# A one-core graph kernel whose edge-count stage is regrouped: five items to a PSUM group, twenty to a set

## The chip, the cores and the metric

The kernel runs on one core of one Trainium2 chip. The metric is device time in microseconds (us) of one execution. The engines are TensorE (PE; its weight loads are listed apart as PEld), VectorE (DVE), ScalarE (ACT), GpSimd (POOL) and the DMA queue that SyncE (SP) issues. TensorE's clock has two levels, 2.4 GHz (granted clock 1.0) and 1.2 GHz (0.5).

## What is computed

Four graph layers run over 3125 nodes with 96 features and 100000 edges, sorted by destination. Every layer reads neighbours only through sums over edges, so the kernel first builds the dense matrix of edge counts and then uses it in all layers:

```python
edge_index = jnp.stack([src, dst])
h = jnp.maximum(_layernorm(x, axis=-1), 0.0)
x = x + _L0_gnn_ref(h, qW, kW, vW, src, dst)            # attention over edges
h = jnp.maximum(_layernorm(x, axis=-1), 0.0)
x = x + _L1_gnn_ref(h, p_t, Wv, bv, edge_weight, edge_index)
h = jnp.maximum(_layernorm(x, axis=-1), 0.0)
x = x + _L2_gnn_ref(h, src, dst, W, b)                  # segment_sum(h[src], dst)
h = jnp.maximum(_layernorm(x, axis=-1), 0.0)
x = x + _L3_gnn_ref(h, edge_index, ...)                 # Chebyshev propagation
# inside L1: a softmax of edge_weight over the edges of one target
seg_max = jax.ops.segment_max(edge_weights, tgt, num_segments=n)
e = jnp.exp(edge_weights - seg_max[tgt])
denom = jax.ops.segment_sum(e, tgt, num_segments=n)
gamma = e / denom[tgt]
```

The change touches only the first stage, which builds the counts `CT` and, beside it, the softmax of the edge weights.

## The kernel before

**The count stage.** The edges lie in 782 chunks of 128, the destinations in 784 windows of `W = 4`. Since the edges are sorted, chunks and windows cross in a staircase of `NI = 1565` items, each one chunk against one window. For an item, VectorE makes two one-hot tiles from the edges' keys (`one_hots`, L408): `oneS`, 128 edges by 128 low parts of the source, and `mov`, 128 edges by 25*4 = 100 columns (high part of the source, destination in the window). TensorE multiplies them (L516), which gives the counts of that item. **A group** is 4 items in a row: they accumulate in one PSUM bank, 25 blocks of 16 columns, each item at an offset that comes from a register. A fifth matmul with the identity (L520, 400 columns) adds what `CT` already holds there, and ScalarE copies the bank back into `CT` (L559). The staircase is cut in two halves, `LH = 792` items apart, and groups g and g+1 belong to different halves, so that only g and g+2 touch the same place: the identity matmul of g waits for the copy of g-2 (semaphore `placed`). There are 392 groups.

**Sets and registers.** A set is two groups, 8 items, whose one-hots are made by one pair of VectorE instructions; there are `SETS = 198`, in `DEEP = 3` buffers: the one-hots of set s wait until set s-3 is counted. The window offsets lie in a small table `wI` in SBUF. Before every fourth group TensorE and ScalarE each execute a TENSOR_LOAD (`load_windows`, L455): 16 words on TensorE, 4 on ScalarE. I call the four groups between two loads a quad.

**What feeds the keys.** Items come in blocks of 128 slots (`NJ = 13`). For block j GpSimd gathers the chunks by indirect DMA (L207, L210), VectorE splits the source (`high`, L416 and L419), GpSimd makes the keys (`keys`, seven instructions, L217 to L229), TensorE transposes them (`turn_items`) and ScalarE stores them (`keep_items`, L543). Tables of numbers say after which set each of this happens (`TURN_AT`, `HIGH_AT`). Where an item's chunk lies is found by comparing slot numbers with the chunks' last windows: VectorE's `past` (L302 for block 0, L433 for the other twelve, in sets 0 to 3) and sums on TensorE (`later_sums`, L476, after sets 3, 4 and 5, 28 matmuls each).

**The softmax** runs on VectorE in 12 steps, one after every eighth set (`SOFT_AT`), each a run of several instructions over 128x782 elements (`soft_step`, L355).

**The start.** `CT` (39350 f32 words a partition) must be zero before the first group; GpSimd, VectorE and ScalarE share that (`ZG1` to `ZA`), and TensorE waits for the semaphores `zero_g`, `zero_v` and `zero_a`. A second iota, `iotaS` for blocks 1 to 12, is written by GpSimd at L234.

After the stage all engines meet (`meet`), and projection, attention, propagation and the last layer follow.

Of the kernel before, what the change touches and what calls it, by code (L numbers as in the profile page):

```python
# [15 lines left out]
NP = 3136  # L16
# [4 lines left out]
NC = 782  # L21
# [3 lines left out]
LH = 792  # L25
NW = NP // W
NI = NC + NW - 1
NJ = 13
# [78 lines left out]
TURN_AT = {14 if j == 1 else 16 * (j - 1) + 6: j for j in range(1, NJ)}  # L107
HIGH_AT = {12 if j == 1 else 16 * (j - 1) + 1: j for j in range(1, NJ)}
SOFT_AT = {24 + 8 * k: k for k in range(1, 13)}


PAST_AT = {0: (0, 1), 1: (2, 3), 2: (4, 5), 3: (6,)}
SUM_AT = {3: range(1, 5), 4: range(5, 9), 5: range(9, NJ)}
SLOTS_AT, TABLE_AT = 8, 10
KA = 5


def items_of(g):
# [10 lines left out]
def keys_of(K, j):  # L129
    return K.KLa[:, j, :, :, :] if j < KA else K.KLb[:, j - KA, :, :, :]  # L130


def alloc_build(K, st):
# [4 lines left out]
    K.KLa = sb(st, "KLa", [128, KA, 2, 128, 2], I16)  # L138
# [23 lines left out]
    K.oneS = sb(st, "oneS", [128, DEEP, 8, 128], F16)  # L162
    K.mov = sb(st, "mov", [128, DEEP, 8, 25 * W], F16)
    K.cs = sb(st, "cs", [128, 4], F32)

    with ExitStack() as st2:
        K.iotaS = sb(st2, "iotaS", [128, SLOTS], I16)
        K.past = sb(st2, "past", [128, 7, SLOTS], F16)
    K.KLb = sb(st, "KLb", [128, NJ - KA, 2, 128, 2], I16)
# [1741 lines left out]
```

## Time and profile before

| | |
|---|---|
| median of 3 runs | 1454.96 us (1450.79 to 1456.13) |
| the profiled execution's own time | 1454.33 us |
| its span in the trace | 1452.3 us |
| PE, DVE, ACT, POOL busy over the span | 79%, 69%, 49%, 37% |
| the count stage in it, first matmul on `oneS` to the last copy | 29.1 to 416.9 us |

The time of an execution holds the span and 2.0 us around it. Busy shares are averages over stages with different limits, so the count stage has to be read by itself: in what rhythm its groups follow one another, and what ends each pause.

### The profile page before, as it was taken

The page shows a single profiled execution, that of the slowest core. Times are in us where ns is not written, and L with a number is a line of the kernel's source. Part 1 is how long each engine was busy: PE and PEld are TensorE (multiplying, and loading weights), DVE is VectorE, ACT ScalarE, POOL GpSimd, SP SyncE. Part 2 cuts the span into 40 slices and gives each one's busy share as a digit, 9 for nine tenths or more (in the row PEclk, how much of TensorE's full clock was granted, in tenths as well). Part 3 has the DMA queues.
Part 4 walks back from the last instruction along what each step waited for, and adds up shares of the span by engine and source line. Part 5 has one row for each costly group of instructions (what it writes and reads, how often), then busy time and mean ns, then how long its engine had stood idle before and what let it go on. Part 6 is the DMA issues. An engine that isn't in the chain of part 4 may idle for free.

```text
span 1452.3 us, 24477 instructions
## 1 busy us (share of the span) xinstructions
PE 1142.7 (79%) x8411; PEld 676.2 (47%) x8411; DVE 1008.8 (69%) x1873; ACT 717.7 (49%) x986; POOL 538.7 (37%) x325
## 2 busy tenths in 40 slices
PE   2877876787769947788787877788479699999994
PEld 1555554555535412122222222222368697778783
DVE  7678788766653438989998999887775554432376
ACT  6555554555532149989997989987100000001121
POOL 6521211221000063989997999887000000000000
PEclk9857666776658959999998999999589899999996
DMA  0100000000013311111111121111111100010111
GB/s 4 55 10 5 5 5 5 16 8 1 1 35 84 95 42 30 43 42 45 44 43 39 32 59 47 50 45 38 50 42 50 37 29 8 1 28 8 50 36 34
DMA packets 61187, 47.32 MB, mean 33 GB/s; under 512 B 31216, under 2 KB 59504, under 8 KB 60944
## 3 DMA queue, kind: packets, MB, share of 16 engines
q1 hardware_dynamic: 59440, 44.04, 10.8%
q0 software_dynamic: 1632, 1.72, 0.5%
q8 instruction: 76, 1.25, 0.4%
q14 instruction: 39, 0.32, 0.1%
HBM read 31.94 MB, written 13.79 MB: 31 GB/s over the span
## 4 chain that ended last, share of the span: by engine, by line
PE 52%; DVE 23%; ACT 15%; issue 6%; POOL 2%; another core or an unknown queue 1%; DMA 0%; ACTq 0%; SPq 0%; DVEq 0%
PE PS L1312 16%; DVE Eb L1118 12%; PE PS L516 10%; PE PS L520 8%; ACT Eb L1083 5%; ACT Eb L1085 5%; ACT CT L559 3%; PE PS L1032 3%; PE PS L1668 3%; PE PS L852 2%; PE PS L1021 2%; PE PS L1042 1%; PE PS L836 1%; POOL Eb L959 1%; DVE Eb L1112 1%
## 5 line engine op out<-in xcount | busy, mean ns | idle before, releaser
L959 POOL TENSOR_SCALAR Eb<-Eb 128x1024 f32<-128x1024 f32 (+4 forms) x164 | 405.1, 2484 | 71.6 <-ACT Eb L1087 71.2
L1118 DVE SCALAR_TENSOR_TENSOR Eb<-Eb,PS 128x1024 f32<-128x1024 f32 (+4 forms) x350 | 365.0, 1083 | 51.6 <-ACT Eb L1085 38.9
L516 PE MATMUL PS<-mov,oneS 128*128 128x100 f16 x1565 | 220.1, 257 | 93.2 <-ACT CT L559 70.9
L559 ACT ACTIVATE CT<-PS 128x400 f32 x392 | 197.6, 504 | 185.7 <-PE PS L520 176.4
L1312 PE MATMUL PS<-hs,CT 128*128 128x192 f16 (+3 forms) x2500 | 270.2, 272 | 6.0 <-DVE B L1513 2.7
L1087 ACT ACTIVATE Eb<-PS,small 128x1024 f32<-128x1024 f32 (+5 forms) x257 | 247.2, 995 | 35.2 <-PE PS L1032 22.6
L1312 PEld LDWEIGHTS PS<-hs,CT 128*128 128x128 f16 (+1 forms) x2500 | 233.5, 101 | 39.2 <-DVE B L1513 3.2
L516 PEld LDWEIGHTS PS<-mov,oneS 128*128 128x128 f16 x1565 | 160.4, 115 | 176.5 <-DVE mov L408 109.0
L1032 PE MATMUL PS<-Qb,Kb 96*128 96x512 f16 (+3 forms) x700 | 202.4, 372 | 25.7 <-ACT Eb L1087 9.9
L520 PE MATMUL PS<-CT,identb 128*128 x392 | 182.6, 466 | 0.9 <-ACT CT L559 0.8
L1042 PE MATMUL PS<-Eb,V 128*25 128x512 f32 (+3 forms) x1400 | 174.8, 572 | 2.1 <-DVE Eb L1118 2.0
L1021 PE MATMUL PS<-identb,CT 128*128 128x128 f16 (+1 forms) x625 | 69.9, 228 | 87.5 <-DVE Eb L1118 83.5
L408 DVE TENSOR_TENSOR oneS<-iotaX,KLb 128x1024 f16<-128x1024 int16 x118 | 82.7, 701 | 66.4 <-PE PS L520 65.4
L1032 PEld LDWEIGHTS PS<-Qb,Kb 96*128 96x128 f16 (+1 forms) x700 | 47.6, 100 | 161.7 <-ACT Eb L1087 84.6
L1021 PEld LDWEIGHTS PS<-identb,CT 128*128 128x128 f16 (+1 forms) x625 | 40.7, 101 | 163.3 <-DVE Eb L1118 149.6
L1083 ACT ACTIVATE Eb<-PS,small 128x1024 f32<-128x1024 f32 (+4 forms) x93 | 102.8, 1105 | 25.8 <-PE PS L1032 14.5
L1513 DVE TENSOR_REDUCE SG<-PS 128x96 f32<-128x288 f32 (+3 forms) x75 | 30.1, 420 | 104.7 <-PE PS L1312 104.3
L1085 ACT ACTIVATE Eb<-Eb,small 128x1024 f32<-128x1024 f32 (+4 forms) x93 | 97.6, 1050 | 3.0
L222 POOL TENSOR_SCALAR key<-hi 128x128 f32<-128x128 int32 x13 | 8.2, 627 | 238.0 <-DVE hi L416 237.8
L1406 ACT ACTIVATE hs<-PS 96x96 f32<-96x96 f32 x9 | 2.2, 248 | 179.1 <-PE PS L1333 179.1
L408 DVE TENSOR_TENSOR oneS<-iotaX,KLa 128x1024 f16<-128x1024 int16 x80 | 56.6, 708 | 38.0 <-PE PS L520 28.9
L1112 DVE TENSOR_SCALAR Eb<-Eb 128x1024 f32<-128x1024 f32 (+4 forms) x93 | 66.2, 712 | 20.3 <-ACT Eb L1087 11.1
(270 smaller groups left out, 1096.1 us busy)
## 6 DMA issues: line engine op xcount, KB each, us to landing
Kb<-kd SPq DMA_DIRECT2D x168, 96.0 KB
qd<-QH SPq DMA_DIRECT2D x24, 96.0 KB, 2.0
kd<-QH SPq DMA_DIRECT2D x24, 96.0 KB, 2.2
XG<-x_d SPq DMA_DIRECT2D x12, 192.0 KB, 2.4
x_d<-XG SPq DMA_DIRECT2D x12, 192.0 KB, 1.9
hs<-t_d SPq DMA_DIRECT2D x12, 192.0 KB, 2.5
Qb<-qd SPq DMA_DIRECT2D x4, 384.0 KB, 3.7
CT<-x_d SPq DMA_DIRECT2D x1, 1200.0 KB, 7.8
```

The lines of the kernel that those rows point to most:

```text
L516: t.matmul(to, K.oneS[:, s % DEEP, 4 * r + k, :], K.mov[:, s % DEEP, 4 * r + k, :].rearrange("p (a w) -> p a w", a=25), start=(k == 0), st ...
L520: t.matmul(ps, K.identb[:, :], K.CT[:, :, bass.ds(vals[0], 4 * W)], start=False, stop=True, skip_group_check=True).then_inc(S("counted"), 1)
L559: a.activation(K.CT[:, :, bass.ds(vals[0], 4 * W)], K.bank(g % 4)[:, 0:25 * 4 * W].rearrange("p (a c) -> p a c", a=25), ACT.Copy).then_inc ...
L959: g.tensor_scalar(e, e, ELO, None, ALU.max).then_inc(S("floored"), 1)
L1021: m = p.transpose(K.cntv[it % 2][0:r, 128 * i:128 * i + w], K.CT[0:w, B0[b] + i, 128 * t:128 * t + r], K.identb[0:w, 0:w])
L1032: m = p.matmul(bank(h)[0:r, 0:wb], K.Kb[:, it % NK, h, 0:r], K.Qb[:, b % 2, h, 0:wb], start=True, stop=True)
L1042: m = p.matmul(bank(4)[32 * h:32 * h + 25, 0:wb], K.V[0:r, t, h, :], K.Eb[0:r, (2 * it + h // 2) % NE_, h % 2, 0:wb], start=(t == 0), stop ...
L1083: a.activation(e, ps, ACT.Relu, bias=K.ten[0:r, 0:1], scale=K.unsc[0:r, :]).then_inc(S("score_read"), 1)
L1085: a.activation(e, e, ACT.Exp, bias=K.ten[0:r, 1:2]).then_inc(S("exp_a"), 1)
L1087: a.activation(e, ps, ACT.Exp, scale=K.unsc[0:r, :]).then_inc(S("score_read"), 1)
L1118: v.scalar_tensor_tensor(out=e, in0=e, scalar=EHI, in1=cn, op0=ALU.min, op1=ALU.mult).then_inc(S("weighed"), 1)
L1312: m = p.matmul(bank(t % FIRST)[0:r, 0:w], K.CT[:, a, 128 * t:128 * t + r], hs[:, a, :, :].rearrange("p k d -> p (k d)"), start=(a == 0), s ...
```

## The change

A group is five items now and a set four groups, twenty items (`GI = 5`, `SET = 20`). The identity matmul has 500 columns, the copy 128x500, the one-hot instructions 128x2560 and 128x2000. There are 313 groups in 80 sets, with two buffers in place of three. A register load belongs to one set: 20 words for four groups of five. A block is 120 slots, and there are 14; the keys lie in a ring of 4 blocks. The wait for `placed` of g-4 is gone (that of g-2 stands). The softmax is dealt out in 27 single pieces by a table of gaps. The comparisons are made in three parts (block 0, blocks 1 to 7, blocks 8 to 13), the second of them before the count loop; the large iota stands before the first gather, where a zeroing of 2000 words stood, and the zeroing shares are new. The halves are `LH = 795` apart.

```diff
-LH = 792
+LH = 795
-NJ = 13
+NJ = 14
-SETS = 198
-SLOTS = NJ * 128
-PRESENT = [g for g in range(2 * SETS) if 4 * (g // 2) + LH * (g % 2) < NI]
-DEEP = 3
-SOFT_AT = {24 + 8 * k: k for k in range(1, 13)}
+GI = 5
+SETS = 80
+SET = 4 * GI
+BLOCK = 6 * SET
+SLOTS = NJ * BLOCK
+PRESENT = [g for g in range(4 * SETS) if GI * (g // 2) < (LH, NI - LH)[g % 2]]
+DEEP = 2
+RING = 4
+HIGH_AT = {3 if j == 1 else 6 * (j - 1) + 1: j for j in range(1, NJ)}
+TURN_AT = {4 if j == 1 else 6 * (j - 1) + 3: j for j in range(1, NJ)}
+PARTS = ((0, 1), (1, 8), (8, NJ))
+PAST_AT = {0: (0, 1, 2, 3), 1: (4, 5, 6)}
+SUM_AT, SLOTS_AT, TABLE_AT = 2, 5, 7
+SOFT_GAPS = (1, 1, 1, 3, 3, 1, 1, 1, 3, 3, 1, 3, 1, 3, 3, 1, 1, 1, 3, 3, 1, 1, 1, 1, 3, 3, 1)
+SOFT_AT = {16 + sum(SOFT_GAPS[:k]): k for k in range(len(SOFT_GAPS))}
...
-ZG1, ZG2, ZG3 = 2000, 5500, 12500
-ZV = ZG3 + 6500
-ZA = ZV + 15000
+ZG1, ZG2 = 3500, 10500
+ZV = ZG2 + 4500
+ZA = ZV + 18500
...
-    g.memset(K.CTf[:, 0:ZG1], 0.0).then_inc(S("zero_g"), 1)
+    g.iota(K.iotaS[:, BLOCK:SLOTS], [[GI, 12 * (NJ - 1)], [LH, 2], [1, GI]], base=GI * 12, channel_multiplier=0,
+           allow_small_or_imprecise_dtypes=True).then_inc(S("iota"), 1)
...
     gather(0)
-    g.memset(K.CTf[:, ZG1:ZG2], 0.0).then_inc(S("zero_g"), 1)
-    g.iota(K.iotaS[:, 128:SLOTS], [[4, SLOTS // 8 - 16], [LH, 2], [1, 4]], base=4 * 16, channel_multiplier=0,
-           allow_small_or_imprecise_dtypes=True).then_inc(S("iota"), 1)
+    g.memset(K.CTf[:, 0:ZG1], 0.0).then_inc(S("zero_g"), 1)
     keys(0)
-    g.memset(K.CTf[:, ZG2:ZG3], 0.0).then_inc(S("zero_g"), 1)
     g.wait_ge(S("slot_w"), 2)
     gather(1)
+    g.memset(K.CTf[:, ZG1:ZG2], 0.0).then_inc(S("zero_g"), 1)
...
+    soft = softmax_pieces(v, K)
     for s in range(SETS):
-        j, o = s // 16, 8 * (s % 16)
+        j, o = s // 6, SET * (s % 6)
         v.wait_ge(S("items"), j + 1)
         if s >= DEEP:
-            v.wait_ge(S("counted"), before(2 * (s - DEEP) + 2))
+            v.wait_ge(S("counted"), before(4 * (s - DEEP) + 4))
...
         if s in SOFT_AT:
-            soft_step(SOFT_AT[s])
+            next(soft)
...
     for g in PRESENT:
-        s, r = g // 2, g % 2
+        s, o = g // 4, GI * (g % 4)
         if g % 4 == 0:
-            quad = load_windows(K, t, mybir.EngineType.PE, g // 4, 1)
-        vals = quad[g % 4]
-        ps = bank(g % 4)[:, 0:25 * 4 * W].rearrange("p (a c) -> p a c", a=25)
-        t.wait_ge(S("one_hot"), s + 1)
-        if g >= 4:
-            t.wait_ge(S("placed"), INDEX[g - 4] + 1)
-        for k in range(items_of(g)):
+            words = vals = to = None
+            words = load_windows(K, t, mybir.EngineType.PE, s, 1)
+            t.wait_ge(S("one_hot"), s + 1)
+        vals = words[g % 4]
+        ps = bank(g % 4)[:, 0:25 * GI * W].rearrange("p (a c) -> p a c", a=25)
+        for k in range(GI):
```

**TensorE, at a register load.** Of before, from the last product of a quad on:

```order
L516 MATMUL PS<-mov,oneS 128x25x4
L520 ISA [waits placed]
L520 MATMUL PS<-CT,identb 128x400
L455 TENSOR_LOAD wI [waits reg_set]
L516 MATMUL PS<-mov,oneS 128x25x4 [waits placed,one_hot]
L516 ISA
```

Of after, the same place (`ISA` is the arithmetic on the registers that a matmul's address needs):

```order
L553 MATMUL PS<-mov,oneS 128x25x4
L557 ISA [waits placed]
L557 MATMUL PS<-CT,identb 128x500
L485 TENSOR_LOAD wI [waits reg_set]
L553 MATMUL PS<-mov,oneS 128x25x4 [waits one_hot]
L553 ISA
```

The sequence is the same, but it stands 80 times in place of 99, and between two loads there are 20 products where there were 16.

**VectorE, at the reciprocal of the softmax.** Of before (the step after set 104):

```order
L408 TENSOR_TENSOR mov<-iotaM,KLb 128x800
L351 COPY cs<-PS 128x1 [waits scan_p]
L353 SCALAR_TENSOR_TENSOR A<-sn,cs,A 128x782 [waits step_v]
L395 RECIPROCAL A<-A 128x782 [waits step_v]
L397 TENSOR_TENSOR A<-wv,A 128x782 [waits step_v]
L332 SCALAR_TENSOR_TENSOR A<-sp,A 128x782 [waits step_v]
L333 TENSOR_REDUCE cs<-sp 128x1
L335 COPY cs<-A 128x1 [waits step_v]
L408 TENSOR_TENSOR oneS<-iotaX,KLb 128x1024 [waits counted,items]
```

Of after (sets 54 to 56):

```order
L302 SCALAR_TENSOR_TENSOR A<-sn,cs,A 128x782 [waits step_v]
L435 TENSOR_TENSOR oneS<-iotaX,KL 128x2560 [waits counted,items]
L435 TENSOR_TENSOR mov<-iotaM,KL 128x2000
L444 TENSOR_SCALAR hi<-GS 120x128 [waits key_turned,key,gs_in0]
L447 SCALAR_TENSOR_TENSOR lo<-hi,GS 120x128 [waits hi]
L355 RECIPROCAL A<-A 128x782 [waits step_v]
L435 TENSOR_TENSOR oneS<-iotaX,KL 128x2560 [waits counted,items]
L435 TENSOR_TENSOR mov<-iotaM,KL 128x2000
L358 TENSOR_TENSOR A<-wv,A 128x782 [waits step_v]
L435 TENSOR_TENSOR oneS<-iotaX,KL 128x2560 [waits counted,items]
```

What was one run of six instructions between two pairs of one-hots is spread over four sets; a block's `high` lies in the same gap as the reciprocal.

**GpSimd, from the small iotas to the second gather.** Of before:

```order
L202 IOTA iotaM 128x100
L204 MEMSET CT 128x2000
L207 DMA GS<-in_src,cI 128x128 [waits slot_w]
L210 DMA GD<-in_dst,cI 128x128
L233 MEMSET CT 128x3500
L234 IOTA iotaS 128x1536
L217 TENSOR_SCALAR dl<-GD,win 128x128 [waits gd_in0]
```

and, behind the keys of block 0:

```order
L229 TENSOR_TENSOR va<-over,key 128x128 [waits step_g]
L237 MEMSET CT 128x7000
L207 DMA GS<-in_src,cI 128x128 [waits slot_w]
L210 DMA GD<-in_dst,cI 128x128
L207 DMA GS<-in_src,cI 128x128 [waits lo,key]
```

Of after:

```order
L196 IOTA iotaM 128x100
L198 IOTA iotaS 128x1560
L202 DMA GS<-in_src,cI 120x128 [waits slot_w]
L205 DMA GD<-in_dst,cI 120x128
L228 MEMSET CT 128x3500
L212 TENSOR_SCALAR dl<-GD,win 120x128 [waits gd_in0]
```

and, behind the keys of block 0:

```order
L224 TENSOR_TENSOR va<-over,key 120x128 [waits step_g]
L202 DMA GS<-in_src,cI 120x128 [waits slot_w]
L205 DMA GD<-in_dst,cI 120x128
L232 MEMSET CT 128x7000
L202 DMA GS<-in_src,cI 120x128 [waits lo,key]
```

The large iota moved ahead of the first gather, and the last zeroing from before the second gather to behind it.

## Rows read from the trace of the kernel before

**Rows 1.** Busy time by stretch: PE, PEld, DVE, ACT, POOL, granted clock, DMA, GB/s.

```profile
29.10:416.90 387.80, 299.91 (x2082) 205.62 (x2082) 281.90 (x476) 203.69 (x405) 85.41 (x108) 0.68 0.03 11
```

**Rows 2.** The same view of two short stretches, one at each clock.

```profile
147.00:153.00 6.00, 4.54 (x31) 3.02 (x30) 4.30 (x10) 3.06 (x7) 0.00 (x0) 0.50 0.00 0
215.00:224.00 9.00, 7.22 (x55) 5.10 (x54) 7.00 (x15) 4.80 (x10) 5.45 (x7) 1.00 0.03 8
```

**Rows 3.** Timeline of PE at half clock: start us, us, engine, line, operation.

```profile
151.07 0.54 PE L520 MATMUL PS<-CT,identb 128*128 x1
152.34 0.61 PE L516 MATMUL PS<-mov,oneS 128*128 128x100 f16 x4 [0.73 <-ACT CT L559]
152.80 0.51 PE L520 MATMUL PS<-CT,identb 128*128 x1
...
154.78 0.53 PE L520 MATMUL PS<-CT,identb 128*128 x1
```

**Rows 4.** The same at full clock.

```profile
216.57 0.34 PE L520 MATMUL PS<-CT,identb 128*128 x1
...
217.22 0.34 PE L520 MATMUL PS<-CT,identb 128*128 x1
218.52 0.56 PE L516 MATMUL PS<-mov,oneS 128*128 128x100 f16 x4 [0.96 <-ACT CT L559]
```

**Rows 5.** Register loads by engine: ns min/median/max, first and last start.

```profile
L455 ACTq TENSOR_LOAD <-wI x99: 884/907/1209, 27.7 to 413.4; - x99
L455 PEldq TENSOR_LOAD <-wI x99: 1101/1107/1512, 27.7 to 412.7; - x99
```

**Rows 6.** Groups of instructions from 30 to 416 us: busy us, mean ns, idle before.

```profile
L559 ACT ACTIVATE CT<-PS 128x400 f32 x391 | 197.0, 504 | 184.9 <-PE PS L520 175.7 <-issue 1.7
...
L408 DVE TENSOR_TENSOR oneS<-iotaX,KLb 128x1024 f16<-128x1024 int16 x118 | 82.7, 701 | 66.4 <-PE PS L520 65.4
L408 DVE TENSOR_TENSOR mov<-iotaM,KLb 128x800 f16<-128x800 int16 x118 | 69.3, 587 | 0.0
```

**Rows 7.** Timeline of PE: first identity matmuls of quads 0, 60 and 97.

```profile
29.55 0.51 PE L520 MATMUL PS<-CT,identb 128*128 x1
...
271.90 0.51 PE L520 MATMUL PS<-CT,identb 128*128 x1
...
411.44 0.51 PE L520 MATMUL PS<-CT,identb 128*128 x1
...
412.71 0.51 PE L520 MATMUL PS<-CT,identb 128*128 x1 [0.42 <-ACT CT L559]
```

**Rows 8.** Timeline around the tenth softmax step, DVE and then PE.

```profile
230.43 1.85 DVE L353 TENSOR_TENSOR_SCAN A<-sn,cs,A 128x782 f32<-128x782 bf16 x1
...
232.31 5.04 DVE L395 RECIPROCAL A<-A 128x782 f32<-128x782 f32 x1
...
242.24 0.61 PE L516 MATMUL PS<-mov,oneS 128*128 128x100 f16 x4 [7.17 <-DVE mov L408]
```

**Rows 9.** Timeline of the first 42 us, four engines, and the sums.

```profile
3.06 1.77 DVE L294 TENSOR_SCALAR lw<-lw 128x7 int32<-128x7 int32 x1 [0.95 <-DMA lw<-in_dst]
...
7.48 1.19 POOL L207 DMA_INDIRECT GS<-in_src,cI  x1 [2.67 <-DVE cI L315]
...
12.89 4.61 POOL L234 IOTA iotaS<- 128x1536 int16 x1
...
21.50 5.93 POOL L237 MEMSET CT<- 128x7000 f32 x1
...
29.10 0.60 PE L516 MATMUL PS<-mov,oneS 128*128 128x100 f16 x4 [6.79 <-issue]
...
35.56 0.93 PE L476 MATMUL PS<-oneh,past 128*128 128x1 f16 x28
```

**Rows 10.** Timeline of PE in the projection stage, the same work at either clock.

```profile
437.67 5.81 PE L836 MATMUL PS<-CT,ones 128*32 128x512 f16 x50
...
467.48 1.89 PE L836 MATMUL PS<-CT,ones 128*32 128x512 f16 x50
```

More of the change, by code:

```diff
@@ new lines, in softmax_pieces @@
+    v.wait_ge(S("edges_in"), 6 * 16)
+    v.tensor_tensor(sp[:, :], dc, prev, ALU.is_equal).then_inc(step, own.up())
+    v.tensor_tensor(sn[:, :], dc, dn, ALU.is_equal).then_inc(step, own.up())
+    yield
+    v.wait_ge(step, own.n)
+    v.tensor_scalar(ie[:, :], sn[:, :], -1.0, 1.0, ALU.mult, ALU.add).then_inc(step, own.up())
+    v.tensor_scalar(A1[:, :], sp[:, :], 1.0, BIG, ALU.subtract, ALU.mult).then_inc(step, own.up())
+    yield
+    scan_a(A1, wv, ALU.add, ALU.max, -BIG, False)
+    yield
@@ new lines, in softmax_pieces @@
+    scan_b(A1, False)
+    yield
+    scan_c(0, ALU.add, ALU.max, -BIG, False)
+    yield
+    scan_e(0, A1, wv, ALU.add, ALU.max, False).then_inc(step, own.up())
+    yield
+    v.wait_ge(step, own.n)
+    v.tensor_tensor(A3[:, :], A2[:, :], ie[:, :], ALU.mult).then_inc(step, own.up())
+    yield
+    scan_a(sn, A3, ALU.mult, ALU.add, 0.0, True)
+    yield
+    scan_b(sn, True)
+    yield
+    scan_c(1, ALU.mult, ALU.add, 0.0, True)
+    yield
+    scan_e(1, sn, A3, ALU.mult, ALU.add, True).then_inc(step, own.up())
@@ new lines, in softmax_pieces @@
+    yield
+    v.wait_ge(step, own.n)
+    v.tensor_tensor(A1[:, :], wv[:, :], A2[:, :], ALU.subtract).then_inc(S("less_max"), 1)
+    yield
+    v.wait_ge(S("edge_exp"), 1)
+    scan_a(sp, wv, ALU.mult, ALU.add, 0.0, False)
+    yield
+    scan_b(sp, False)
+    yield
+    scan_c(2, ALU.mult, ALU.add, 0.0, False)
+    yield
+    scan_e(2, sp, wv, ALU.mult, ALU.add, False).then_inc(step, own.up())
+    yield
+    v.wait_ge(step, own.n)
+    v.tensor_tensor(A3[:, :], A2[:, :], ie[:, :], ALU.mult).then_inc(step, own.up())
@@ new lines, in softmax_pieces @@
+    yield
+    scan_a(sn, A3, ALU.mult, ALU.add, 0.0, True)
+    yield
+    scan_b(sn, True)
+    yield
+    scan_c(3, ALU.mult, ALU.add, 0.0, True)
+    yield
+    scan_e(3, sn, A3, ALU.mult, ALU.add, True).then_inc(step, own.up())
+    yield
+    v.wait_ge(step, own.n)
+    v.reciprocal(A1[:, :], A2[:, :]).then_inc(step, own.up())
+    yield
+    v.wait_ge(step, own.n)
+    v.tensor_tensor(A3[:, :], wv[:, :], A1[:, :], ALU.mult).then_inc(step, own.up())
+    yield
+    scan_a(sp, A3, ALU.mult, ALU.add, 0.0, False)
@@ L445, in build_vector, with load_windows @@
+        if s == TABLE_AT:
+            table(2)
         if s in SOFT_AT:
-            soft_step(SOFT_AT[s])
+            next(soft)
     v.wait_ge(step, own.n)
-def load_windows(K, e, ety, q, every):
-    j, o = q // 8, 16 * (q % 8)
-    row = K.wI0[0:1, o:o + 16:every] if j == 0 else K.wI[j - 1:j, o:o + 16:every]
-    e.wait_ge(K.S("reg_set"), 1 if j == 0 else 2)
+def load_windows(K, e, ety, s, every):
+    j, o = s // 6, SET * (s % 6)
+    h = 0 if j == 0 else 1 if j < PARTS[2][0] else 2
+    r = j - PARTS[h][0]
+    e.wait_ge(K.S("reg_set"), h + 1)
```

363 lines of the change are left out of this document (163 added, 200 removed).

## The prediction, made before the changed kernel was run

> **What bounds the kernel now.** I read the busy time by stretch first, then the timeline of the count stage, then the register loads, the groups of instructions and the start. The diff touches only the count stage, 387.8 us of the span, in which PE is busy 77%, DVE 73%, ACT 53% at a mean granted clock of 0.68 [rows 1]. No engine is full, so the rhythm has to be read. Between the identity matmuls of neighbouring groups lie 0.65 to 0.66 us: 1.98 us for three groups at half clock [rows 3], 0.65 us at full clock [rows 4]. The clock hardly shows, because two limits happen to be equal. At 1.2 GHz a group streams 4 x 100 + 400 = 800 columns, 0.667 us. At 2.4 GHz that would be half, but five matmuls with a weight load each still take 0.64 to 0.65, 0.13 apiece. After the fourth group of a quad the next product starts 1.27 us behind the identity matmul at half clock and 1.30 at full clock [rows 3, 4], where within a quad it is 0.33. That pause is the TENSOR_LOAD: 1.107 us on TensorE's queue, 99 times [rows 5]. VectorE does not set it: the one-hots of a set take 0.70 + 0.59 [rows 6] and lie ready. The first group after a load is paced by its weight loads, 0.46 us from first product to identity matmul [rows 3].
>
> A quad is therefore 3 x 0.66 + 0.46 + 1.27 = 3.71 us by its parts. Measured over the 37 quads from 271.90 to 411.44, where no softmax step is left, it is 3.771 [rows 7]; the 0.06 more are key turns and the moments at which the clock changes. All 97 quads from 29.55 to 411.44 take 381.9 us, and 97 x 3.771 = 365.8, so 16.1 us are stalls of another kind. The largest lies behind the reciprocal: 5.04 us inside one run of VectorE work that began with the scan at 230.43, and PE idle for 7.17 us until 242.24 [rows 8].
>
> **The change part by part.**
>
> *The quad becomes a set of 20 items.* At half clock a group streams 5 x 100 + 500 = 1000 columns, 0.833 us, +0.167 for each of the three that follow closely. The first group has one product more at the pace of its weight loads, 0.46/4 = +0.115. At full clock there are six matmuls at 0.13, +0.128 each for three groups, and again +0.115. The pause of 1.27 us holds the identity matmul, 100 columns longer, beneath the load, so it grows only by the load's own length. ScalarE's load of 4 words takes 0.907 and TensorE's of 16 takes 1.107 [rows 5]; if the difference is the words, one costs 0.0167 us, and 20 words cost +0.067. The difference could also be the engines', so the bounds are 0 and the whole load by the word, 1.107/16 x 4 = 0.28; I take 0.067, between them and the only slope that two rows give. Together +0.683 at half clock and +0.566 at full clock; the mean clock of 0.68 [rows 1] is 36% at full clock, so +0.64, and a set is 3.771 + 0.64 = 4.41 us for 20 items, 0.221 an item against 0.236.
>
> *ScalarE and the way round.* The copy of 400 columns takes 0.504 [rows 6]. Per column I take the half-clock TensorE price, 0.083 us for 100, which gives 0.587 for 500 columns and about 0.75 with the 0.16 between copies: under 0.833 at half clock, equal to the six matmuls' 0.77 at full clock. The way round from the identity matmul of g-2 over its copy to that of g is 1.27 us where nothing else is in the way, in the last groups [rows 7]; with 0.17 added it is 1.44 for two groups, below two groups' 1.67. The wait on g-4 that is removed is covered by the one on g-2 and costs and gives nothing.
>
> *VectorE with two buffers.* Two points, 1024 elements in 0.701 us and 800 in 0.587 [rows 6], are 0.51 ns an element and 0.18 fixed. 2560 and 2000 elements then take 1.49 and 1.20, with their overlap of some 0.1 about 2.6 us a set. VectorE may begin set s when set s-2 is counted, and TensorE then still has the whole of s-1 before it, 4.41 us, with the load at its start and another before s. So VectorE is idle 1.8 us a set, and it can be late by another 2.3 before TensorE notices (4.41 + about 0.5 of the next pause - 2.6). Work up to 1.8 us a set is free, and a single piece up to 4.1.
>
> *The softmax pieces.* Every piece but one is a scan of 1.85 us with a small copy, 2.0, or less [rows 8]: free. The reciprocal falls in set 55 with a block's `high` (about 0.5): 5.04 + 0.5 + 0.2 left over = 5.8, which is 1.7 over what is free. Of the 16.1 us of stalls, 2.1 were the early sums (quads 1 and 2 of [rows 7]'s stretch, by their part) and 14.0 the softmax; 1.7 are left. Bounds: 0, and all 14.0 again if the cover is not there.
>
> *The sums.* 28 matmuls take 0.93 us [rows 9] before a load; 42 come after set 2: 1.0 us beyond what the load hides (bounds 0 and 1.4). The other 49 stand before the loop, under the start. The key turns and softmax turns now all stand right before a load, whose 1.1 us hides their 0.3 to 0.4: nothing.
>
> *The start.* At 3.06 a VectorE instruction on seven elements takes 1.77 us, until GpSimd's zeroing of 2000 words ends [rows 9]: the one held the other up. Now the iota of 1560 stands there, 4.61/1536 x 1560 = 4.68 us from about 2.9, so `lw` ends near 7.65 in place of 4.83 and the first gather starts at 10.3 in place of 7.48 (+2.8). Behind it the iota is missing: zeroing 3500 words at 5.93/7000 a word is 3.0, so after two gathers (1.19 each and a gap) GpSimd comes to the keys at 15.8 in place of 17.3, and they end near 20.0 in place of 21.5 [rows 9]. But then come two gathers, 2.4, before the zeroing of 7000 words, 5.93: it ends at 28.4 in place of 27.4, and the first product stands 1.67 behind, as before (29.10 - 27.43): 30.1, +1.0. Bounds: 0, and +4 if the seven comparisons of 840 elements, newly placed beside the first gather, and GpSimd's work exclude each other as `lw` and the zeroing did.
>
> *The tail.* One half has five groups left, which follow one another by the way round: 1.44 twice, 1.44 + 0.52 = 1.96 twice where a load lies between, and 1.30 to the end of the last copy: 8.1 from the first identity matmul. Before, four groups took 416.9 - 411.44 = 5.5.
>
> *The sum.* First identity matmul 30.1 + 0.575 = 30.7; 77 full sets at 4.41 are 339.6; reciprocal 1.7, sums 1.0, tail 8.1: the stage ends at 381.1, not 416.9, **35.8 us less**. Against the profiled execution's own 1454.33 that is 1418.5 us. Its median of runs is 1454.96, 0.04% away. The stages behind are the same instructions. Their clock need not be: 50 matmuls of the projection take 5.81 us at half clock and 1.89 at full clock [rows 10], and that stage starts at half clock now.
>
> One rule speaks against the change. The Trainium skill, "Runtime: NRT & Kernel Launch", section "Instruction fetch mechanics", says of TENSOR_LOAD that a register costs about 200 ns, in bulk too. It speaks of loads from HBM; here the table lies in SBUF, and 16 words took 1.107 us [rows 5], where 16 x 200 ns would be 3.2, so the trace does not bear it out. By that price four words more would be an estimated +0.8 us a set, and the time about 1474.
>
> **The rivals.**
> - *The stalls stay.* With two buffers VectorE's extras could reach TensorE at once. The idle time in the rows and the single pieces speak against it. If 14.0 us stay in place of 1.7: 1430.8.
> - *The clock.* All sets at half clock would be +0.04 x 77 = 3 us, all at full clock -0.08 x 77 = -6; the projection's dips can move by 4 us for each piece of [rows 10]. That gives about 1409 or 1429. For it: the clock in the stage switches every few us [rows 2]. Against: both clocks give nearly the same rhythm.
> - *A load paid by the word.* 0.28 in place of 0.067 for the four words, 80 times: +17, 1435.5. Against it: 4 words on ScalarE take 0.907, not a quarter.
> - *VectorE becomes the pace, slower than before.* The one-hots are read at 0.51 ns an element. If the longer instructions lost that and ran at half the rate, a set would take 4560 x 1.02 + 0.3 = 5.0 us on VectorE; 80 sets are 400, and the softmax (about 41 us of work) and `high` (7) would all lie on the path: the stage would end near 475, the time near 1512. It decides from 4.3 us a set on (80 x 4.3 + 48 + the start is the present stage); 2.6 is measured out of two sizes of the same instruction, on the same types and pattern. So it is far.
> - *It does not do what it says.* If the pause is not the load but the wait for `placed` or the one-hots, it would come 4 groups apart all the same, and only the softmax would gain; but the load's 1.107 and the pause's 0.94 above the pace fit too closely.
>
> **How the numbers follow.** Forecast 0.64 (own range 1412 to 1426), the stalls stay 0.10, clock 0.14 (both sides), load by the word 0.04, VectorE the pace 0.04, something like no change 0.04. The likeliest is 1418.5. The range 1407 to 1433 takes in the forecast, the clock and the stalls, with the bounds of start (+3) and sums. Half a percent, 7 us, is about what a measurement of this kernel can tell from no change; all cases but the last two gain more. Faster 0.91, the same 0.04, slower 0.05.
>
> **What would show it.** In the changed profile: 80 loads of about 1.17 us; identity matmuls 0.83 apart at half clock and 0.77 at full clock; a set of 4.41 us; a pause of 1.34 after each load; one-hots of 1.49 and 1.20 us; the longest wait of TensorE for VectorE 1 to 3 us, at the reciprocal; the first product at 30 us, the last copy at 381. Wrong would be a load of 1.4 us or more, one-hots of over 2 us, PE idle before a load's group for longer than 1.3 us in most sets, or a first product beyond 34 us.

## The result, and the profile after

The changed kernel takes 1392.65 us (median of 4 runs, 1391.74 to 1393.33), the kernel before on the same chip 1452.91 (1450.79 to 1456.13). The ratio is 0.9583, with a 95% interval of 0.956 to 0.9606. That is 60 us less, where 36 were forecast, and 14 us below the lower end of the range: the sign is right and the size is not.

| profiled execution | before | after | forecast |
|---|---|---|---|
| its own time | 1454.3 | 1392.3 | 1418.5 |
| first product on `oneS` | 29.1 | 30.65 | 30.1 |
| last copy ends | 416.9 | 361.7 | 381.1 |
| from there to the end of the span | 1035.4 | 1028.9 | no change |

So 19.4 of the 26 us that the forecast is off lie in the count stage. The other 6.5 lie behind it, in instructions that nobody changed. Measured from the first matmul of the projection, 0.4 us behind the last copy, that part varies between 1028 and 1041 us in the profiles of before, after and e1 to e8, so I draw nothing from it.

The busy time of the count stage of after, to compare with [rows 1]: busy us of PE, PEld, DVE, ACT and POOL, then the granted clock. It was 0.68, and is 0.85:

```profile
30.65:361.70 331.05, 259.42 (x1963) 165.97 (x1963) 254.39 (x241) 190.40 (x327) 118.03 (x114) 0.85 0.04 12
```

The register loads of after, for [rows 5]: ns min/median/max, first and last start. TensorE's grew from 1107 to 1360 ns:

```profile
L485 ACTq TENSOR_LOAD <-wI x80: 884/895/1149, 29.0 to 359.1; - x80
L485 PEldq TENSOR_LOAD <-wI x80: 1356/1360/1548, 29.0 to 358.4; - x80
```

The groups of instructions of after from 31 to 340 us, for [rows 6]. The copies and one-hots have the forecast lengths (0.587; 1.49 and 1.20 were forecast for the one-hots). ScalarE and VectorE wait for TensorE, hardly ever the other way round:

```profile
L553 PE MATMUL PS<-mov,oneS 128*128 128x100 f16 x1479 | 175.3, 232 | 64.4 <-issue 61.1 <-DVE mov L435 2.7
L593 ACT ACTIVATE CT<-PS 128x500 f32 x295 | 173.1, 587 | 133.9 <-PE PS L557 125.7 <-issue 0.2
...
L435 DVE TENSOR_TENSOR oneS<-iotaX,KL 128x2560 f16<-128x2560 int16 x74 | 111.4, 1505 | 65.7 <-PE PS L557 63.8 <-ACT KL L578 1.7
L435 DVE TENSOR_TENSOR mov<-iotaM,KL 128x2000 f16<-128x2000 int16 x74 | 91.6, 1238 | 0.0
```

The timeline of PE in after at half clock, the first sets, for [rows 3]. Identity matmuls (L557) stand 0.81, 0.84 and 0.83 apart, and 1.25 us after the last of the set the next product starts:

```profile
31.21 0.59 PE L557 MATMUL PS<-CT,identb 128*128 x1
...
32.02 0.62 PE L557 MATMUL PS<-CT,identb 128*128 x1
...
32.86 0.62 PE L557 MATMUL PS<-CT,identb 128*128 x1
...
33.69 0.62 PE L557 MATMUL PS<-CT,identb 128*128 x1
34.94 0.91 PE L553 MATMUL PS<-mov,oneS 128*128 128x100 f16 x5 [0.63 <-issue]
```

And at full clock, for [rows 4]. They stand 0.66, 0.65 and 0.61 apart; one product more in every group, and the pace is still the 0.65 of the kernel before. The pause, from the last identity matmul of a set to the next product, is 303.65 - 302.21 = 1.44:

```profile
300.29 0.39 PE L557 MATMUL PS<-CT,identb 128*128 x1
...
300.95 0.39 PE L557 MATMUL PS<-CT,identb 128*128 x1
...
301.60 0.39 PE L557 MATMUL PS<-CT,identb 128*128 x1
...
302.21 0.39 PE L557 MATMUL PS<-CT,identb 128*128 x1
...
303.65 0.71 PE L553 MATMUL PS<-mov,oneS 128*128 128x100 f16 x5 [1.05 <-issue]
```

To compare kernels I divide the sets (or quads) by the length of their identity matmuls: for 500 columns 0.39 us is full clock and 0.60 half, for 400 it is 0.34 and 0.51. From the first identity matmul (31.21) to that of the tail (353.62), the 77 full sets of after take 4.187 us each.

| medians, full clock / half clock | set | pause | groups at full clock |
|---|---|---|---|
| before, quad of 16 | 3.73 / 3.77 | 1.30 / 1.28 | 32% |
| after, set of 20 | 4.06 / 4.33 | 1.44 / 1.25 | 69% |
| forecast for after | 4.34 / 4.45 | 1.34 | 36% |

Two things went better than forecast: the full-clock set is 0.28 us shorter, and twice as many groups run at full clock.

### The profile page after: what moved, and what is told of

Read it like the earlier page. It is cut to its first block, busy times and chain, and to the rows that moved or that the text cites. A ratio compares the mean times of both kernels' runs of the same rounds, so it can differ in the third digit from the quotient of the medians.

```text
span 1390.6 us, 23439 instructions
## 1 busy us (share of the span) xinstructions
PE 1101.8 (79%) x8345; PEld 640.9 (46%) x8345; DVE 986.4 (71%) x1647; ACT 706.9 (51%) x908; POOL 572.0 (41%) x332
## 4 chain that ended last, share of the span: by engine, by line
PE 52%; DVE 21%; ACT 13%; issue 9%; POOL 2%; another core or an unknown queue 1%; DMA 0%; SPq 0%; DVEq 0%; ACTq 0%; POOLq 0%
PE PS L1346 17%; DVE Eb L1152 12%; PE PS L553 10%; PE PS L557 7%; ACT Eb L1117 6%; ACT Eb L1119 5%; PE PS L1702 3%; PE PS L1066 2%; PE PS L886 2%; PE PS L1055 2%; PE PS L870 1%; POOL Eb L993 1%; PE PS L1337 1%; ACT Eb L1121 1%
## 5 line engine op out<-in xcount | busy, mean ns | idle before, releaser
L1152 DVE SCALAR_TENSOR_TENSOR Eb<-Eb,PS 128x1024 f32<-128x1024 f32 (+4 forms) x350 | 365.1, 1083 | 46.6 <-ACT Eb L1119 31.4
L593 ACT ACTIVATE CT<-PS 128x500 f32 x313 | 183.7, 587 | 144.6 <-PE PS L557 135.9
L553 PE MATMUL PS<-mov,oneS 128*128 128x100 f16 x1565 | 185.7, 231 | 77.2 <-issue 73.9
L553 PEld LDWEIGHTS PS<-mov,oneS 128*128 128x128 f16 x1565 | 146.8, 107 | 159.4 <-issue 116.7
L1066 PE MATMUL PS<-Qb,Kb 96*128 96x512 f16 (+3 forms) x700 | 198.1, 365 | 25.3 <-issue 11.1
L1076 PE MATMUL PS<-Eb,V 128*25 128x512 f32 (+3 forms) x1400 | 170.8, 560 | 2.9 <-DVE Eb L1152 2.9
L435 DVE TENSOR_TENSOR oneS<-iotaX,KL 128x2560 f16<-128x2560 int16 x80 | 120.3, 1504 | 72.3 <-PE PS L557 70.4
L557 PE MATMUL PS<-CT,identb 128*128 x313 | 142.8, 456 | 1.1 <-ACT CT L593 0.9
L1547 DVE TENSOR_REDUCE SG<-PS 128x96 f32<-128x288 f32 (+3 forms) x75 | 30.1, 420 | 104.4 <-PE PS L1346 104.0
L435 DVE TENSOR_TENSOR mov<-iotaM,KL 128x2000 f16<-128x2000 int16 x80 | 98.8, 1234 | 0.0
L217 POOL TENSOR_SCALAR key<-hi 120x128 f32<-120x128 int32 x14 | 8.8, 628 | 176.8 <-DVE hi L444 176.7
```

Source lines behind the costliest of these rows:

```text
L435: return v.tensor_tensor(out.rearrange("p e (c two) -> p e c two", two=2), v_in, k_in, ALU.is_equal)
L553: t.matmul(to, K.oneS[:, s % DEEP, o + k, :], K.mov[:, s % DEEP, o + k, :].rearrange("p (a w) -> p a w", a=25), start=(k == 0), stop=False ...
L557: t.matmul(ps, K.identb[:, :], K.CT[:, :, bass.ds(vals[0], GI * W)], start=False, stop=True, skip_group_check=True).then_inc(S("counted"), 1)
L593: a.activation(K.CT[:, :, bass.ds(words[g % 4][0], GI * W)], K.bank(g % 4)[:, 0:25 * GI * W].rearrange("p (a c) -> p a c", a=25), ACT.Copy ...
L1066: m = p.matmul(bank(h)[0:r, 0:wb], K.Kb[:, it % NK, h, 0:r], K.Qb[:, b % 2, h, 0:wb], start=True, stop=True)
L1076: m = p.matmul(bank(4)[32 * h:32 * h + 25, 0:wb], K.V[0:r, t, h, :], K.Eb[0:r, (2 * it + h // 2) % NE_, h % 2, 0:wb], start=(t == 0), stop ...
```

## The experiments

Every kernel here computes everything. The quoted paragraph before each result is what was expected before that run. Times are medians; "the kernel before" is run beside each on its own chip.

**What a second wait costs.** Reading the trace of before again, behind the result, shows a row that the prediction passed over: the instructions of one line on TensorE's queue (PEldq), ns min/median/max.

```profile
L513 PEldq EVENT_SEMAPHORE  x388: 51/51/51, 32.7 to 414.5; - x194
```

A group's first matmul waited for `one_hot` and for `placed` of g-4. Here 388 of the 392 groups (all but the four that have no g-4) show one wait as an instruction of its own. It never takes longer than 51 ns, so the wait was always met already. In after the row is gone. My theory after the result: this wait, satisfied long before, is what cost time, and the rival: it is harmless, and the gain comes from the larger groups. e1 puts both waits back into the changed kernel, e2 takes them out of the old one.

```diff
 # e1, from the changed kernel
         vals = words[g % 4]
         ps = bank(g % 4)[:, 0:25 * GI * W].rearrange("p (a c) -> p a c", a=25)
+        t.wait_ge(S("one_hot"), s + 1)
+        if g >= 4:
+            t.wait_ge(S("placed"), INDEX[g - 4] + 1)
 # e2, from the kernel before
-        t.wait_ge(S("one_hot"), s + 1)
-        if g >= 4:
-            t.wait_ge(S("placed"), INDEX[g - 4] + 1)
+        if r == 0:
+            t.wait_ge(S("one_hot"), s + 1)
```

> The changed kernel with the two waits of before in front of every group on TensorE: for the set's one-hots, and for the copy of g-4. Both are met long before, so they only cost their execution. Theory A (the waits paced the groups at full clock before, 0.64 us where five matmuls need less): at full clock a step from group to group grows from 0.65 to 0.72-0.75 us, a set from 4.06 to 4.3-4.4, the full-clock share falls, and the time goes from 1393 to 1405-1418. Theory B (the waits cost nothing, as the prediction held, and the full-clock pace comes from ScalarE's copies): step 0.65, time 1391 to 1395.

Measured: 1424.3 us (1422.76 to 1430.66), ratio to before 0.9809 (0.9766 to 0.9853), 32 us slower than the changed kernel. That is more than either theory allowed (at most 1418). The row is back, 309 times; its longest, 1036 ns, is a real wait:

```profile
L553 PEldq EVENT_SEMAPHORE x309: 51/51/1036, 35.0 to 390.4; - x155
```

A full-clock set takes 4.51 us in place of 4.06, with 0.78 between identity matmuls in place of 0.65; a half-clock set 4.56 in place of 4.33, with the same 0.83 between identity matmuls and a pause of 1.51 in place of 1.25. Groups at full clock fall from 69% to 48%.

> The kernel before without the wait for the copy of g-4 and with the wait for the one-hots only once a set. Theory A: the full-clock step falls from 0.645 to 0.55-0.60, a quad at full clock from 3.73 to about 3.5, and the time by 5 to 15 us. Theory B: nothing moves, 1451 to 1455.

Measured: 1419.69 us (1416.86 to 1422.3), ratio 0.977 (0.9732 to 0.9808), 31 us faster than before, where Theory A had said 5 to 15. A full-clock quad takes 3.31 us in place of 3.73, and identity matmuls stand 0.5 to 0.6 apart; 84% of the groups run at full clock. The stalls of the softmax, which the old rhythm had partly covered, now stand out: 97 quads take 346.1 us, some 25 more than 97 x 3.31. Both directions give the same 31 to 32 us, or 33 by the ratios.

e5 and e6 ask whether it is a wait in each group or the second one, by putting back only one of the two, from the second group of a set on.

```diff
 # e5, from the changed kernel
+        if g % 4:
+            t.wait_ge(S("one_hot"), s + 1)
         for k in range(GI):
 # e6, from the changed kernel
+        if g >= 4 and g % 4:
+            t.wait_ge(S("placed"), INDEX[g - 4] + 1)
         for k in range(GI):
```

> The changed kernel with only the wait for the one-hots put back in front of the second to fourth group of each set: one wait at the group's first matmul, not two. In the profile of before, and of the run with both waits back, the second wait of a matmul stands as a semaphore instruction of its own on TensorE's queue, 388 times 51 ns. Theory A1 (only that separate instruction costs, a first wait rides on the matmul): no such instruction, full-clock steps of 0.65, time 1391 to 1396. Theory A2 (each wait costs by itself): half of the 31 us, 1403 to 1412.

> The changed kernel with only the wait for the copy of g-4 put back, in the second to fourth group. Theory A1: as after, 1391 to 1396. Theory A2: 1403 to 1412. Theory A3 (it is this wait that really holds TensorE up, because the copy of g-4 is late): 1415 to 1425, and the trace shows ScalarE's copy of g-4 ending just before the group's first matmul.

Measured: 1396.58 us (1393.8 to 1400.48), ratio 0.9608 (0.9585 to 0.9632), and 1394.61 (1388.8 to 1396.09), ratio 0.9589 (0.9558 to 0.9619). No instruction of its own appears in either, full-clock sets take 4.03 and 4.00 us, and the count stages of the two profiles take 327.7 and 328.6 us, where that of after takes 331.1. So one wait rides on the matmul and costs nothing that can be told; only the second becomes an instruction. On the row it has 51 ns, but on the pace it weighs 0.13 us (0.65 to 0.78); why it weighs more than its row, no run shows.

**The clock.** e4 asks how much of the remaining half-clock share is to be had: two matmuls of 512 columns, whose result nobody uses, before each register load.

```diff
         if g % 4 == 0:
             words = vals = to = None
+            if s:
+                for _ in range(2):
+                    t.matmul(bank(5)[:, 0:512], K.identb[:, :], K.warm[:, :], start=True, stop=True)
             words = load_windows(K, t, mybir.EngineType.PE, s, 1)
```

> The changed kernel with two useless 512-column matmuls (constants, a free PSUM bank) behind each set, in front of the register load, so that TensorE works while its sequencer loads. Their result is not used. Theory C (the clock is granted by how much TensorE has done, and the load's pause is what lets it fall): granted clock in the stage from 0.84 to near 1.0, sets of 4.1 us throughout, the projection starts at full clock; time 1378 to 1388. Theory D (the clock does not follow this, and the matmuls lie in the way): clock as it was, a set 0.2 to 0.4 us longer, time 1405 to 1425.

Measured: 1393.09 us (1391.28 to 1397.6), ratio 0.9583 (0.9548 to 0.9617): no difference in the time, and neither theory's. But the clock of the stage did rise, and the stage was 7 us shorter. The busy time from 31 to 340 us, of after and then of e4 (granted clock: the third number from the end):

```profile
31.00:340.00 309.00, 244.43 (x1858) 156.82 (x1856) 241.03 (x231) 179.36 (x308) 117.68 (x114) 0.86 0.04 12
```

```profile
31.00:340.00 309.00, 264.93 (x2048) 161.62 (x2047) 247.03 (x235) 182.87 (x314) 118.31 (x114) 0.99 0.04 13
```

The stages behind took 12 us more in that one execution. To tell whether this is chance, I ran the same kernel again beside the changed one, both in five rounds.

> The changed kernel with two unused matmuls of 512 columns before each register load (as e4), beside the changed kernel itself on the same chip, both in five rounds. In the profile its count stage was 7 us shorter, yet the time the same. If the 7 us are really gained and the later stages only fell badly in that one execution: 1386 to 1389, against 1392 to 1393 for the changed kernel. If the later stages pay it back each time: within 2 us of the changed kernel.

> The changed kernel itself, for e11 to be compared with and as a second profile of it: 1392 to 1394 us, count stage 330 to 333 us; if the share of groups at full clock (69%) is a property of the kernel and not of one execution it is 60 to 75% again, and the attention stage, the same instructions, shows by how much a stage varies from one execution to another (up to 10 us in the profiles so far).

Measured: e11 1375.03 us (1371.59 to 1377.63), ratio 0.9584 (0.9559 to 0.9609); e12 1379.16 (1376.38 to 1382.41), ratio 0.9618 (0.9593 to 0.9643). This chip is faster as a whole: the kernel before takes 1432.96 here, and the attention stage, from its first score matmul to its last, takes 480 to 485 us in each of the profiles of e9 to e12, where it took 493 to 505 in before, after and e1 to e8. So only ratios, or differences on this chip, are to be used. The dummy matmuls bring 4.1 us by the medians: of the 36 pairs of one run of e11 and one of e12, one stands the other way round, though the intervals of the two ratios overlap. In the two profiles the count stage is 7.0 us shorter with the dummies (325.7 and 332.7), and what lies behind it is 2.6 us longer (1017.1 and 1014.5). Full-clock shares are 63% in e12 (69% in the first profile, 60 to 75% expected) and 97% in e11. So the version with the dummies is ahead of the changed kernel where both ran on one chip, by a margin that e4, beside the kernel before alone, could not show.

**The softmax.** e7 lumps the 27 pieces of the changed kernel into 12 steps, one every fourth set, as the kernel before had them.

```diff
-SOFT_AT = {16 + sum(SOFT_GAPS[:k]): k for k in range(len(SOFT_GAPS))}
+LUMPS = ((0, 4), (4, 5), (5, 9), (9, 10), (10, 12), (12, 14), (14, 15), (15, 19), (19, 20), (20, 25), (25, 26), (26, 27))
+SOFT_AT = {16 + 4 * k: k for k in range(12)}
...
-            next(soft)
+            for _ in range(*LUMPS[SOFT_AT[s]]):
+                next(soft)
```

> The changed kernel with the 27 softmax pieces gathered again into the 12 steps of before, one after every fourth set from 16 on. By the prediction's arithmetic VectorE is idle 1.5 to 1.8 us a set and has about 2 more in the buffer; the steps have 5.4, 5.6, 2.9, 5.7 and 10.8 us of work, and what goes beyond 3.7 falls on TensorE: 1.7 + 1.9 + 2.0 + 7.1 less the stall of 2 us that stands now, about 11 us: 1401 to 1406. Rival (dealing out is worth nothing, as the buffers take it anyway): 1391 to 1396.

Measured: 1404.62 us (1403.74 to 1410.5), ratio 0.9684 (0.9654 to 0.9713): 12 us slower than the changed kernel. In the profiles TensorE's waits for VectorE in the stage grow from 2.7 us to 15.1 (8.8 for `mov`, 6.3 for `cs`), that is by 12.4; the stage itself is 7 us longer (338.0 and 331.1), with 75% of its groups at full clock. The size was forecast from the stalls of before, as 14.0 - 1.7 = 12.3.

e9 makes the cross-check: the kernel before, with its groups of four and sets of eight, without the second wait (e2) and with the softmax dealt out, one piece every fifth set.

```diff
 # e9, from e2
-SOFT_AT = {24 + 8 * k: k for k in range(1, 13)}
+SOFT_AT = {32 + 5 * k: k for k in range(27)}
...
         if s in SOFT_AT:
-            soft_step(SOFT_AT[s])
+            next(soft)
```

> The kernel before (groups of four, sets of eight, three buffers, its own start), without the wait on g-4 and with one wait per set for the one-hots as in e2, and now also with the softmax dealt out in the 27 pieces of the changed kernel, one after every fifth set from set 32. It computes everything. The kernel with the waits alone took 1419.7 us. If the waits and the dealing are nearly the whole gain: the quads already run at 3.31 us at full clock, 98 of them are 325 to 335 us with the starts of blocks, the count stage takes 335 to 340 us and the time is 1400 to 1406. If groups of five and sets of twenty are what hides the softmax (two sets of eight ahead are less cover than one of twenty): the pieces still stall TensorE, count stage 345 or more, time 1412 or more.

Measured: 1383.99 us (1382.87 to 1384.51), ratio 0.9649 (0.962 to 0.9679), where e12, on the same chip, has 0.9618. These two edits alone bring 49.0 us of e12's 53.8, and the count stage takes the 335 to 340 us that were expected (336.1). The five items, the sets of twenty, the new start and the early sums bring the other 5, and the intervals overlap. In the two profiles only 1.8 of these 5 lie before the last copy (365.1 and 363.3). (By ratios, dealing out is worth 0.977 - 0.9649, 17.6 us, here, and 12 in e7.)

**Five items and twenty words.** e3 is the changed kernel with four items to a group and sixteen to a set.

```diff
-LH = 795
-NJ = 14
+LH = 792
+NJ = 17
...
-GI = 5
-SETS = 80
+GI = 4
+SETS = 99
```

> The changed kernel with four items to a group and sixteen to a set (99 sets, 17 blocks of 96 slots), everything else as after. If the fifth item is what counts: 98 sets of about 3.7 us instead of 77 of 4.19, the stage about 40 us longer, time 1425 to 1435, and the granted clock in the stage back near 0.7. If the waits and the softmax pieces are what counts: 98 x 3.5 = 343, about 20 us longer than after, time 1408 to 1418.

Measured: 1410.38 us (1405.86 to 1413.26), ratio 0.9712 (0.9677 to 0.9748), 18 us slower than the changed kernel. The time is inside the second forecast, but the profile puts only a part of the 18 us down to the rhythm: the first product stands at 36.6 in place of 30.65, the stage is 335.9 us in place of 331.1, and what lies behind it, in the profile, is 3 us longer, which is within its variation. The late start is no matter of four items. The comparisons beside the first gather even take less than in after (2.25 and 2.55 us). What is longer is one instruction of GpSimd's second gather, and the zeroing of 7000 words, for which TensorE waits, stands behind it: it begins at 29.19 in e3 and at 22.99 in after. The timeline of POOL in e3, and then in after:

```profile
21.62 7.57 POOL L205 DMA_INDIRECT GD<-in_dst,cI  x1 [0.30 <-issue]
```

```profile
22.01 0.98 POOL L205 DMA_INDIRECT GD<-in_dst,cI  x1 [0.30 <-issue]
```

In e3 VectorE is busy from 21.49 to 28.38 without a pause, from just ahead of this instruction to just before its end; in after its next one-hots begin at 22.50, behind it. That the two exclude each other here is my guess; no run tests it. A full-clock set of 16 takes 3.32 us, 0.2075 an item, against 4.06/20 = 0.203: the five items are worth 0.0045 x 1565 = 7 us at equal clock. Against it, 95% of e3's groups run at full clock. From the first identity matmul on, 97 quads take 330.4 us in e3 (37.05 to 367.46) and 330.3 in e9 (29.55 to 359.83), so that at four items to a group the larger sets and the new feeding of the keys bring nothing to the rhythm.

e10 is the register load alone: the kernel before with 20 words on TensorE, four of them unused.

```diff
-    row = K.wI0[0:1, o:o + 16:every] if j == 0 else K.wI[j - 1:j, o:o + 16:every]
+    n_ = 16 if every > 1 else 20
+    row = K.wI0[0:1, o:o + n_:every] if j == 0 else K.wI[j - 1:j, o:o + n_:every]
```

> The kernel before, with TensorE's register load of 20 words in place of 16 (four more that nobody uses), ScalarE's as it was. The load alone, without the larger groups. The load will take 1.36 us in place of 1.11, as in the changed kernel. If each load stands on the path by its whole length: 98 x 0.25 = 25 us more, 1476 to 1480. If it lies partly beside the identity matmul at half clock, where the pause of the changed kernel hardly grew: 5 to 15 us more, 1458 to 1468. By the prediction's 0.067 a load: 1459.5 at most.

Measured: 1459.01 us (1456.56 to 1462.53) against 1432.96, ratio 1.0183 (1.0151 to 1.0216): 26 us slower, and the pause is 1.55 us at full clock and 1.54 at half clock, where before it is 1.30 and 1.28: 98 x 0.25 is 24.5 of the 26. The expectations were written against a before of 1453; as differences they were +25, +5 to +15, and at most +6.6, and the first holds.

```profile
L458 PEldq TENSOR_LOAD <-wI x99: 1356/1363/1931, 27.7 to 435.2; - x99
```

The load has the length that it has in the changed kernel, and the whole of the 0.25 us stands on the path.

**A load ahead of the identity matmul.** e8 moves TensorE's load of the next set's words before the last identity matmul of a set, so that the load would lie beside products that are still running.

```diff
+        v0 = vals[0]
+        if g != PRESENT[-1] and g // 4 != PRESENT[INDEX[g] + 1] // 4:
+            words = vals = to = None
+            words = load_windows(K, t, mybir.EngineType.PE, s + 1, 1)
         if g >= 2:
             t.wait_ge(S("placed"), INDEX[g - 2] + 1)
```

> The changed kernel with TensorE's register load of the next set in front of the last identity matmul of the set instead of behind it, so that the five products of that group run while the sequencer loads. If the pause is the load (1.36 us) less what TensorE has queued: about 0.4 us less a set, 77 x 0.4 = 30 us, 1360 to 1370. Rival (the last group's copy then comes later and ScalarE or the way round over CT takes its place): gain under 10 us, 1383 to 1395.

Measured: 1427.63 us (1424.8 to 1430.59), ratio 0.9822 (0.9796 to 0.9848), 35 us slower, which neither forecast had. Its timeline of PE and ACT around one such load, at half clock before it and full clock behind:

```profile
200.39 0.60 PE L561 MATMUL PS<-CT,identb 128*128 x1
...
202.43 0.39 PE L561 MATMUL PS<-CT,identb 128*128 x1 [1.02 <-ACT CT L597]
...
203.66 0.39 PE L561 MATMUL PS<-CT,identb 128*128 x1
...
203.99 1.07 ACT L597 ACTIVATE CT<-PS 128x500 f32 x2 [0.47 <-issue]
...
204.71 0.39 PE L561 MATMUL PS<-CT,identb 128*128 x1 [0.31 <-ACT CT L597]
```

The pause did not shrink, it moved: 2.04 us from identity matmul to identity matmul, as long as pause and first group together were (1.44 + 0.61). The move laid something else bare: ScalarE's own load of 0.89 us used to end beneath TensorE's. Now its first copy of the set is late (203.99, after "issue"), and the identity matmul of two groups on waits for it: 204.71 - 203.66 = 1.05 us in place of 0.65. A full-clock set takes 4.33 us, and 52% of the groups run at full clock in place of 69%. That ScalarE's load is what costs the 35 us is read from this trace; no run moved that load too.

## Why the forecast was wrong, step by step

**The step that failed** is the sentence "The wait on g-4 that is removed is covered by the one on g-2 and costs and gives nothing". It asked only whether the wait is ever unsatisfied, and it never is. What it costs is the instruction: e1 and e2 put its price at 31 to 32 us. The prediction's own sum prices a kernel that keeps this instruction, and that kernel exists: it is e1. It took 1424.3 us, where the forecast was 1418.5. The change also reduced the wait for `one_hot` from every group to one a set, which the prediction did not price at all; by e5 and e6 either of the two waits could have stayed without cost. This one step is worth more than the whole error of 26 us on the changed kernel; the other errors went the other way.

**The same error stands in the account of the pace.** "Five matmuls with a weight load each still take 0.64 to 0.65, 0.13 apiece" took the full-clock pace for weight loads. Without the semaphore instruction five take 0.5 to 0.6 (e2, e3) and six take 0.65 (after), some 0.11 apiece. The forecast of 0.77 for six is what e1 shows, 0.78. A pace divided by the wrong number of instructions still fitted before perfectly, since it was made from it.

**The clock** was forecast to keep its share of 36%. It went to 69%, and it follows the same cause: 32% before and 84% in e2, 69% after and 48% in e1. The rival "The clock" allowed 6 us if all sets were at full clock, because both levels then seemed to give nearly the same rhythm. Once the instruction is gone they no longer do: 4.06 against 4.33. Why the clock is granted more often then is not shown; e4 and e11 show only that matmuls in the pause bring it to 96 and 97%.

**The load by the word** was given 4 chances in 100, at +17 us, and it is how the load behaves: 1.107 us for 16 words and 1.360 for 20, 0.063 a word, where I took 0.0167. The choice of slope was the error: it came from two engines (4 words on ScalarE, 16 on TensorE). By TensorE's own two sizes the part that does not grow with the words is 0.10 us; if ScalarE had the same slope, its part would be 0.64. The forecast pause of 1.34 hides two errors that nearly cancel. In e9, with the old load and without the second wait, the pause is 1.19 at full clock and 1.15 at half clock, so 0.11 to 0.13 of the old pause was the wait's instruction too. With 0.25 for the four words that makes 1.44 at full clock, which is what after shows, and 1.40 at half clock, where it shows 1.25. There 0.15 of the load is hidden. I read that so: at half clock TensorE takes 0.83 us for what its queue issues in 0.65, so that the queue is ahead when it comes to the load. This is argued, not shown. With the second wait back, the queue needs 0.78 for a group and the pause at half clock is 1.51 (e1), which fits; in e9 it needs 0.53 for what TensorE does in 0.66, and yet only 0.04 is hidden, which does not. e8, which tried to use it, gained nothing. The rule that the prediction weighed, from the Trainium skill ("Runtime: NRT & Kernel Launch", "Instruction fetch mechanics"), about 200 ns a register, is not what happens with a table in SBUF: 63 ns a word here. Of a load from HBM, of which the rule speaks, no run here has a row.

**Right:** the half-clock rhythm within a set (0.83), copies of 0.587 and one-hots of 1.50 and 1.24, the tail of 8.1 us (361.7 - 353.62), and the softmax. For the copies there was luck in it: their price a column was borrowed from TensorE. The reciprocal stalls TensorE by 2.7 us, where 1.7 was forecast, and the softmax is worth 12 us (e7), where 12.3 was; by e2 and e9 it is 17.6. In the timeline of after, of DVE and PE around it:

```profile
258.31 5.03 DVE L355 RECIPROCAL A<-A 128x782 f32<-128x782 f32 x1
...
263.26 1.46 DVE L435 TENSOR_TENSOR oneS<-iotaX,KL 128x2560 f16<-128x2560 int16 x1
...
265.98 0.70 PE L553 MATMUL PS<-mov,oneS 128*128 128x100 f16 x5 [2.70 <-DVE mov L435]
```

**The start** came out within 0.6 us (30.65, forecast 30.1). The timeline of its first 9 us shows the mutual exclusion, POOL and DVE, against [rows 9]:

```profile
2.91 5.07 POOL L198 IOTA iotaS<- 128x1560 int16 x1
3.01 4.99 DVE L389 TENSOR_SCALAR lw<-lw 128x7 int32<-128x7 int32 x1
```

Seven elements take 4.99 us because they wait inside the instruction for GpSimd's iota to end at 7.98. The Trainium skill ("SBUF — State Buffer", "SBUF: two separate sides") calls this an exclusive lock on a shared pair of ports, held for a whole instruction; the trace agrees here, with 4.99 us for seven elements. Of VectorE's instructions the page names those in a 2-port mode or with two SBUF inputs; this one has one input, and the trace does not show its mode. The comparisons beside the first gather, for which the bound of +4 us was held open, took 2.55 us for 840 elements x 7 and moved nothing.

**The sum again, with what was measured.** 77 sets at 4.06 and 4.33, 69 to 31, are 77 x 4.14 = 319; stalls and changes of the clock are the other 3 up to 322.4. Against 77 x 4.41 + 2.7 = 342.3 of the forecast this is 20 us, and with the start (+0.5) it is the 19.4 by which the stage ends earlier. Of the 60 us in all, the second wait is some 31, dealing out the softmax 12, and five items with twenty words about 7 at equal clock. What is left, some 10, is the variation of the stages behind (6.5) and what these runs do not separate, the early sums among it. On the other chip the account comes out with less for the rest: the two edits of e9 are 49.0 us of 53.8, and everything else together 5. The parts were measured one at a time, and they need not add up exactly: the second wait also hides some of the softmax's stalls (e2).

## What to carry to other kernels

Before a removed wait is priced at nothing because it is always satisfied, look for it as a row of its own in the queue: one wait is carried by the instruction, a second one is an instruction, and in a rhythm of 0.65 us it is a fifth. Count every instruction of that queue into a pace, semaphores and register work too. A slope belongs to one engine: take it from two sizes on the same engine, or keep the whole load by the word as the value and not as a rival.

## What the runs showed of the hardware that I had not expected

- A matmul with two waits puts an EVENT_SEMAPHORE of 51 ns on TensorE's queue, and the group becomes 0.13 us longer at full clock (0.65 to 0.78) for 51 ns of it in the rows. With either wait alone there is no such instruction and no measurable cost (e5, e6).
- A TENSOR_LOAD from SBUF costs 63 ns a word on TensorE (1.107 us for 16 words, 1.360 for 20), and ScalarE's of 4 words costs 0.895.
- TensorE's granted clock in the same stage differed with what stood in its queue: 0.75 with the second wait, 0.86 without it, 0.97 in groups of four, 0.99 with dummy matmuls in the pause (31 to 340 us of e1, after, e3 and e4).
- Two chips differed by 1.4% in the kernel before, and in the changed kernel by 12.8 us between two profiled executions: the attention stage took 13 us less (493.2 and 480.1), the count stage 1.6 us more (331.1 and 332.7). So ratios and not times carry from one batch of runs to the next.
